# Routed experts of one fused transformer step: f32 products against three f16 products of two-part operands

## What is computed

```python
logits = xt @ gate_w.T
_, idx = jax.lax.top_k(logits + beta, K)                      # K = 2 of E = 8
probs = jax.nn.sigmoid(jnp.take_along_axis(logits, idx, axis=-1))
c = jnp.zeros((B, E), xt.dtype).at[jnp.arange(B)[:, None], idx].add(probs)
g = jnp.einsum('bh,ehm->bem', xt, gate_proj_w)
u = jnp.einsum('bh,ehm->bem', xt, up_proj_w)
h = jax.nn.silu(g) * u
eo = jnp.einsum('bem,emh->beh', h, down_proj_w)
combined = jnp.einsum('beh,be->bh', eo, c)                    # + the shared expert, every token
```

## Time and profile before

| | us |
|---|---|
| time before, median of 3 runs | 3458.92 (3457.98 to 3466.2) |
| span of the profiled execution | 3454.1 |
| PE busy in it | 3251.6 (94%) |
| DVE busy | 2715.8 (79%) |
| ACT busy | 2222.3 (64%) |
| POOL busy | 1600.3 (46%) |
| first stage, to its last product | 0 to 304 |
| second stage, from its first transpose to its last product | 312 to 756 |

### The profile page before, as it was taken

The page is one execution under the profiler, slowest core; times in us unless marked ns, Lnnn a source line. Parts: engine busy times, 40 slices in busy tenths (PEclk is TensorE's granted clock), DMA queues, the critical chain, the costliest instruction groups (busy, mean ns, idle before and its releaser), DMA issues. The chain is left out here.

```text
span 3454.1 us, 59006 instructions
## 1 busy us (share of the span) xinstructions
PE 3251.6 (94%) x19214; PEld 1316.3 (38%) x19215; DVE 2715.8 (79%) x4886; ACT 2222.3 (64%) x3468; POOL 1600.3 (46%) x2080
## 2 busy tenths in 40 slices
PE   8998999999999999999999999778999999999987
PEld 5655666652222222222222222252334334333333
DVE  5564222559999999999999999366989999898997
ACT  3331222127888888888878888757877777777763
POOL 2124000003444343344444443306888888887885
PEclk9999999999999999999999999988999999999998
DMA  4443111111121111111111110041222222222221
GB/s 156 133 163 114 47 45 44 42 42 30 35 60 41 39 38 33 31 32 31 34 36 35 35 36 23 30 141 59 71 74 69 82 73 69 74 83 69 76 77 50
DMA packets 160884, 211.56 MB, mean 61 GB/s; under 512 B 32324, under 2 KB 108364, under 8 KB 160604
## 3 DMA queue, kind: packets, MB, share of 16 engines
q1 hardware_dynamic: 141340, 172.51, 16.6%
q0 software_dynamic: 8512, 18.76, 1.7%
q10 hardware_dynamic: 10752, 16.78, 1.5%
HBM read 154.48 MB, written 52.69 MB: 60 GB/s over the span
## 5 line engine op out<-in xcount | busy, mean ns | idle before, releaser
L1289 ACT ACTIVATE prob<-psS 128x1024 f32<-128x1024 f32 (+3 forms) x1280 | 1104.1, 906 | 275.2 <-PE psS L1473 265.6
L1339 DVE TENSOR_REDUCE pmax<-psR 128x1 f32<-128x512 f32 x1674 | 1057.0, 684 | 76.9 <-PE psR L1415 46.6
L2115 POOL TENSOR_TENSOR hc<-h_d,crep 128x512 f32<-128x512 f32 x512 | 647.3, 1272 | 187.1 <-DVE h_d L2344 136.8
L1415 PE MATMUL psR<-kslab,qslab 48*128 48x512 bf16 (+3 forms) x2480 | 651.9, 351 | 22.2 <-DVE pmax L1339 13.8
L1488 PE MATMUL psVo<-prob,vaug 128*32 128x512 f32 (+3 forms) x5120 | 627.1, 543 | 1.7 <-ACT ov L1293 0.9
L1473 PE MATMUL psS<-qslab,kslab 51*128 51x512 bf16 (+3 forms) x2560 | 531.8, 352 | 39.5 <-ACT prob L1289 24.0
L2344 DVE TENSOR_TENSOR_SCAN h_d<-a,state,psU 128x512 f32<-128x512 f32 x384 | 489.4, 1275 | 0.0
L1204 POOL TENSOR_SCALAR_AFFINE_SELECT prob<-prob 128x256 f32<-128x256 f32 (+1 forms) x512 | 213.4, 420 | 529.0 <-ACT prob L1289 529.0
L1415 PEld LDWEIGHTS psR<-kslab,qslab 48*128 48x128 bf16 x2480 | 187.3, 94 | 627.9 <-DVE pmax L1339 468.7
L2334 DVE TENSOR_TENSOR psU<-dtx,psX 128x512 f32<-128x512 f32 x512 | 356.2, 696 | 88.9 <-PE psX L2494 38.5
L2247 ACT ACTIVATE a<-dt,a_neg 128x512 f32<-128x512 f32 x512 | 366.8, 724 | 53.8 <-DVE h_d L2344 53.0
(11 more groups left out here) (309 smaller groups left out, 4805.5 us busy)
## 6 DMA issues: line engine op xcount, KB each, us to landing
crep<-c_rows_d SPq DMA_DIRECT2D x256, 256.0 KB, 3.2
x_e<-rows_d SPq DMA_DIRECT2D x72, 128.0 KB, 2.0
y_d<-y SPq DMA_DIRECT2D x72, 128.0 KB, 1.7
q_d<-parts SPq DMA_DIRECT2D x48, 128.0 KB
k_d<-parts SPq DMA_DIRECT2D x48, 128.0 KB
qslab<-q_d SPq DMA_DIRECT2D x60, 96.0 KB
kslab<-k_d SPq DMA_DIRECT2D x60, 96.0 KB
x<-in_L_attn_x_dram SPq DMA_DIRECT2D x8, 512.0 KB, 6.3
```

The costliest lines, as they stand in the source:

```text
L1289: act.activation(prob[g % BUFS][:, :, off:BLK], psS[g % 2][:, :, off:BLK], ACT.Exp).then_inc(prob_ready, 1)
L1339: dve.tensor_reduce(into[:, lo:lo + (count - 1) * NEXT + 1:NEXT], psR[at % BANKS][:, 0:count * w].rearrange("p (n w) -> p n w", w=w), AX.X ...
L1415: ins = pe.matmul(dst[:, m * w:(m + 1) * w], qslab[u][rows, i * P:(i + 1) * P], kslab[u][rows, ch * BLK:ch * BLK + w], start=(m == 0), sto ...
L2115: pool.tensor_tensor(hc[:, g % CR], h[:, g % HR], crep[:, g // PAIR % SPR], ALU.mult).then_inc(hc_ready, 1)
```

## The change

Each f32 product of the routed experts becomes three f16 products: x and h are cut into a high and a low f16 part after their transpose, the weights in the first stage, and high*high + high*low + low*high is summed in PSUM. f16 needs a scale: each weight matrix is scaled by its own largest magnitude, x by 1024, and the factors are taken out again in SiLU's scale, in the product h and in the routing weights `c`.

In the first stage every block now handles one expert's weights. ACT loads them into one buffer `raw` (three DMAs, after `copy_values` of the block before, once POOL is through with the last ones). DVE takes their maxima (`weight_max`, ahead of `choose`), PE turns the maxima (`turn_max`, between the two first products), DVE builds a diagonal (`weight_row`), PE spreads it (`spread_max`, ahead of `product(u,0)`), DVE makes the scales (`weight_scale`). ACT writes the high parts and scales `raw` in place (six instructions of 128x1024 a block), and POOL subtracts to get the low parts (three of 128x1024 a block, `low_weights`, behind the scatters). `cut` has four instructions instead of five. x is loaded straight into `xn`. The zeros for the regions' tails are made by POOL after its last low part.

```diff
+            def low_weights(e):
+                for w, low in enumerate((keep["wgl"], keep["wul"], keep["wdl"])):
+                    high = (keep["wgh"], keep["wuh"], keep["wdh"])[w]
+                    pool.wait_ge(whigh_ready, 3 * e + w + 1 + CREDIT)
+                    pool.tensor_tensor(low[:, e].rearrange("p k m -> p (k m)"), raw[:, w],
+                                       high[:, e].rearrange("p k m -> p (k m)"), ALU.subtract).then_inc(wlow_ready, 1)
...
+                low_weights(n)
                 pool.wait_ge(scattered, 16 * 2 * TPB * (n + 1))
...
-                c.after(dve.tensor_tensor(rest[:], rest[:], parts[:, s, 1], ALU.subtract))
-                dve.tensor_copy(parts[:, s, 2], rest[:]).then_inc(parts_ready[s], 1)
+                dve.tensor_tensor(parts[:, s, 2], qf[:, s], parts[:, s, 1], ALU.subtract).then_inc(parts_ready[s], 1)
...
+            def weight_max(e):
+
+                dve.wait_ge(raw_in, 48 * e + 48 + CREDIT)
+                dve.tensor_reduce(wmax[:], raw[:], AX.X, ALU.max, apply_absolute_value=True).then_inc(wscale_step, 1)
...
             def load_expert(e):
+                act.wait_ge(wlow_ready, 3 * e + CREDIT)
...
+            def turn_max(e):
+                pe.wait_ge(wscale_step, 3 * e + 1 + CREDIT)
+                pe.wait_ge(y_ready, e + CREDIT)
+                pe.transpose(psWT, wmax[:], keep["ident"][:]).then_inc(wmax_moved, 1)
+
+            def spread_max(e):
+                pe.wait_ge(wscale_step, 3 * e + 2 + CREDIT)
+                pe.matmul(psWB, ones[0:3, :], diag_r[:], start=True, stop=True).then_inc(wmax_moved, 1)
...
             def step(i, s):
                 take_max(i, 0)
+                if known(i - 1, 0):
+                    dve.wait_ge(hTh_ready, i + CREDIT)
+                    dve.tensor_tensor(hTl[:, 1 - s], psH[:], hTh[:, 1 - s], ALU.subtract).then_inc(hTl_ready, 1)
+                if known(i + 1, 0):
+                    dve.wait_ge(xTh_ready, i + 2 + CREDIT)
+                    dve.scalar_tensor_tensor(out=xTl[:, 1 - s], in0=psX[:], scalar=X_TOP, in1=xTh[:, 1 - s],
+                                             op0=ALU.mult, op1=ALU.subtract).then_inc(xTl_ready, 1)
                 take_max(i, 1)
...
+            def split_products(dst, high, low, w_high, w_low, first, last):
+
+                pe.matmul(dst, high, w_high, start=first, stop=False)
+                pe.matmul(dst, high, w_low, start=False, stop=False)
+                return pe.matmul(dst, low, w_high, start=False, stop=last)
```

More of the change, by code:

```diff
@@ L423, in _ @@
             for n in range(NBLK):
+                weight_max(n)
                 choose(n)
                 cut(n, 0)
+                weight_row(n)
                 cut(n, 1)
@@ L560, in product @@
                     else:
[L561 removed]
+                        w = (wsg if kind == "g" else wsu)[:, k, x * P:(x + 1) * P]
                     ins = pe.matmul(psR[bank][:], w, xnT[n % 2][:, k], start=(k == 0), stop=(k == KD - 1))
@@ L594, in _ @@
                 product(n, "q", 0)
+                turn_max(n)
                 product(n, "q", 1)
                 product(n, "g", 0)
+                spread_max(n)
                 product(n, "u", 0)
@@ L665, in phase_experts @@
         psY = ps("psY", [P, D])
-        psM = ps("psM", [P, BLK])
+        MAX_BANKS = 3
+        psM = [ps(f"psM{s}", [P, BLK]) for s in range(MAX_BANKS)]
         qz = [sb(f"qz{a}", [P, T], BF16) for a in range(2)]
@@ L851, in step @@
                 take_max(i, 2)
-            steps(dve, step, -1, RT + 1)
-            lc = Chain(dve, lam_step)
+                if isinstance(i, int) and i == 2:
+                    scale_outputs()
+            steps(dve, step, -1, RT)
             dve.wait_ge(lam_load, 64 + CREDIT)
             lv = lam_in[:].rearrange("p (m w) d -> p m w d", w=2)
-            lc.after(dve.tensor_tensor(lam_w[:], lv[:, :, 0], lv[:, :, 1], ALU.mult))
-            lc.after(dve.tensor_reduce(lam_s[:], lam_w[:], AX.X, ALU.add))
+            fc.after(dve.tensor_tensor(lam_w[:], lv[:, :, 0], lv[:, :, 1], ALU.mult))
@@ L859, in _ @@
+            fc.after(dve.tensor_reduce(lam_s[:], lam_w[:], AX.X, ALU.add))
         @block.tensor
         def _(pe):
-            pe.wait_ge(keep["moe_w"], 16 * 3 * E)
             def max_product(i, slot):
@@ L913, in step @@
                     ins.then_inc(d_done, 1)
                 max_product(i, 2)
-                if known(i - 1, 0):
-                    pe.wait_ge(h_ready, i + CREDIT)
-                    if known(i - 1, 1):
-                        pe.wait_ge(hT_ready, i - 1 + CREDIT)
-                    for m in range(MT):
-                        ins = pe.transpose(psH[:, m], h[:, 1 - s, m * P:(m + 1) * P], keep["ident"][:])
-                    ins.then_inc(h_turned, 1)
-            steps(pe, step, -1, RT + 1)
+            steps(pe, step, -1, RT)
```

296 lines of the change are left out of this document (186 added, 110 removed).

## The result

The changed kernel takes **3516.0 us** (median of 4 runs, 3510.7 to 3522.3) against 3459.6 (4 runs, 3458.0 to 3466.2) for the kernel before, run beside it: ratio 1.0163, 95% interval 1.0145 to 1.0181. It is slower by 1.6%. Forecast were 3489 us, +0.9%, and a range that ended at 3512: the sign is right, the size is not.

What follows compares the result with a forecast made beforehand. PE was taken to set the pace in both edited stages. Profiled span 3454.1 + 64 + 2 + 43 - 79 = 3484 us; with the runs' median 4.8 above it, 3489 us (+0.9%), range 3434 to 3512.

Steps and rivals of the forecast that it cites:

- Second stage: Second stage's loop: f16 products shorten tiles to 4.6 us and steps with maxima to 5.6; -79 us in all.
- start and tail: Second stage's two ends: the start comes out even, the part after the last gate gains 3 us.
- The weights' load: First stage: PE waits 6.0 us a block for the weights' maximum, plus 3.2 for the spread; 9.2 x 7 = +64 us.
- the spread: First stage, PE's second wait, before spread_max: an extra 2.6 or 3.5 us a block, taken as 3.2.
- DVE's chain: First stage: choose, cut(0) and weight_row end 6.1 us after the maximum, against PE's two products of 3.5 us.
- the low clock: First stage, behind the wait for the maximum: PE's two products may not have the full clock; 3.5 us extra.
- The first block: First stage: the first block's load is issued at the start and competes with x's; +2 us.
- POOL beside DVE: First stage: POOL's low parts hold up DVE's cut(n,3) ahead of down; 5.4 x 8 = +43 us.
- the taking of turns: In cut(3), DVE and POOL instructions alternate: cast waits 1.1, subtraction 2.2, cast 2.2; 5.4 us a block.
- the hold-up: POOL's low parts delaying cut(3): full 38%; rivals none 27% (same sum without 43) and casts only 12% (23 us).

Runs made afterwards that it cites:

- e3: Changed kernel with both moves: next expert's load issued ahead of the copies, POOL's low parts behind hidden(n,3); 3430.8 us, ratio to the kernel before 0.9905.
- e11: e7 with the weights' maximum taken in two instructions, the first two thirds while the last third loads; 3389.2 us, ratio to the kernel before 0.9793.
- e1: Changed kernel with ACT issuing the load of expert n+1 before copy_shared(n) and copy_values(n), not behind them; 3466.1 us.
- e7: e6 with each load third issued after its own low part, turn_max behind the logits, weight_row ahead of choose, spread_max one product earlier; 3411.5 us.
- e4: Changed kernel with POOL waiting for each low part's own completion before it issues the next; 3513.6 us.
- e12: Changed kernel with the first cast of cut(n,3) made to wait for a tiny POOL memset right ahead of the low parts; 3524.1 us.
- e9: Changed kernel with six surplus products put into PE's wait before down, their output overwritten by down; 3497.0 us.
- e6: e3 with the tails' zeros in the free half of xn, not the weights' buffer, so tail stores don't wait for the last low parts; 3422.7 us.
- e8: Changed kernel with twelve surplus products put into PE's wait before down, their output overwritten by down; 3519.4 us.
- e2: Changed kernel with POOL's three low parts waiting until DVE has finished hidden(n,3); 3455.2 us.
- e5: Changed kernel with each of POOL's low parts written as two instructions of 512 columns, without a wait between them; 3525.8 us.
- e10: Changed kernel with the first cast of cut(n,3) written as eight casts of 64 columns; 3526.5 us.

## Why the prediction was right and where it failed

**Second stage, -79 forecast, -83.1 measured: right.** 4.69 us a tile against 4.6; 5.44 a step with maxima against 5.6; start and tail -7.0 against -3, since the last tiles run 4.2 us shorter, not 3, and the first three 2.8 shorter, not even.

**The weights' load, +64 forecast, 46.0 + 17.5 = 63.5 measured: right**, with the parts as worked out: the reduction took 3.35 us (3.5), all landed 6.6 us after the issue at 173.8 (5.5), PE waited 6.6 (6.0), the spread cost 2.5 (3.2). Of the two values that I gave for the spread, 2.6 for DVE's chain and 3.5 for the low clock, the first was the nearer: e3 shows 2.1 of the 2.5 with PE waiting at the full clock. The 3.5 was an estimate, that both products run at the low clock to their end, and no run shows it: behind the wait for `wmax` the granted clock is 0.50 for 2.8 to 6.0 us in the changed kernel (0.50 too in the kernel before from 310 to 318 us, between the two stretches of the earlier trace rows), and from the product on `wmax` to the one on `diag_r` are 5.75 to 6.61 us there and no more in any run, 2.1 to 3.0 above the 3.64 of e11. The first block lost 3.4, not 2. e1 shows that the 46.0 come from the place of the load. Most of the 17.5 doesn't: it came back there as the wait for `diag_r` (10.7 us), since `weight_row` stood behind `choose` and `cut(n,0)`, and went only with e7's order.

**POOL beside DVE, +43 forecast.** The idle time before `down` rose by 44.4 us, so the number held, but partly by accident: the taking of turns that I wrote ("cast waits 1.1, subtraction 2.2, cast 2.2") is what e4 shows, with gaps; in the changed kernel one instruction waits for all three, 6.4 us longer than alone, of which 5.5 reach PE. The low parts took 2.13 us each (2.2 assumed). The term was an estimate from the scatters' 1.21 us against 1.013, which are no arithmetic. The trace agrees with it in that one of the engines waits for whole instructions of the other, but not for one at a time: it shows 6.86 us for three in a row. The rows don't show that the order decides: in all eight blocks the held DVE instruction starts 0.04 to 0.28 us before POOL's first low part, and yet DVE is the one that waits. Starts on POOL are rough in a profile, so these distances say little by themselves, but in e12 the cast waits for a memset ahead of the low parts, starts 0.2 us behind the first of them, and is held as well (6.38 us).

One stage of the kernel before does have arithmetic on both engines, and I hadn't used it. In the last one 512 DVE products with one input in PSUM (`psU<-dtx,psX`, 128x512) run nearly all beside POOL's f32 products of 1.27 us, and none takes over 0.70 us. In e4's last block `hidden`, which also reads PSUM, takes its usual 0.69 beside a low part. What is held in these runs is casts and two-input instructions whose inputs all lie in SBUF.

**The step that failed is the missing term behind it.** For the wait for `wmax` I had asked what 6 us of idleness do to the granted clock, from the earlier trace rows, and priced the products behind it. For the wait before `down`, which my own sum made just as long (1.4 + 5.4 = 6.8 us), I asked nothing and took `down` at its 7.17 us. It took 10.05 in the block shown, 19.0 us more in all eight. e9 fills that wait and `down` loses 17.3 of the 19.0; that its median gains 19.1 is a coincidence, since only 14.3 of it arise before the second stage.

With 19.0 from there, 5.2 that I had entered at nothing (the sixteen small products, 3.8, and a remainder), 2.8 from the hold-up and the first block, and +11.7 in the later stages, against the second stage's 3.4 more of gain (-83.1 + 0.7 for its start, -79 forecast) and 0.5 on the load, the 3484 of the forecast span become the 3519 measured. By the medians the forecast was 27 us low, 4 us outside its range; the clock term alone would have brought it to 3508, inside it.

**The later stages, +11.7.** Their instructions are the same. 7.9 lie in the last stage, from its first product on `pick` to the end: 1104.9 us before, 1112.8 after. But this value follows no edit: it is 1104.8 to 1105.0 in the kernel before, e6, e8, e9 and e11, 1112.6 to 1113.1 in the changed kernel, e1, e2, e3, e5, e7 and e12, 1109.8 in e4 and 1111.3 in e10. It arises at three places of the stage, about 150, 287 and 693 us after its start, with 2 to 3.5 us each. At the first of them the same short waits of PE stand in both runs; then the clock is at 0.50 for some 3.4 us in one and for some 10 in the other (stretches of 2 us added up). Stretches of 20 us there, the same work in each (the number before the last two is the clock), kernel before and kernel after:

```profile
2489.20:2509.20 20.00, 17.33 (x80) 7.04 (x81) 18.61 (x21) 18.19 (x37) 14.93 (x13) 0.91 0.21 73
```
```profile
2546.20:2566.20 20.00, 17.86 (x67) 6.22 (x65) 17.42 (x20) 15.50 (x34) 14.32 (x12) 0.74 0.18 58
```

So about 8 us of any comparison of two profiled runs here can be this, and it is no cost of the change. It may be in the medians as well: the changed kernel's four times are 3510.7, 3511.4, 3520.7 and 3522.3, and the profiled one is the third; the others' stages weren't recorded. The other 3.9 lie between the first attention product and the last stage, 1588.7 us before and 1590.4 to 1593.6 in the changed kernel and every variant; I have not followed them.

**What decides the change.** The f16 products bring their 83 us; the way in which the weights were split gave back 135. With the split placed elsewhere (e11) it gives back about 9 (the second stage's first gate is at 322.8 against 313.7), and the same change is 2.1% faster.

## What to carry to other kernels

Price a wait of the engine that sets the pace twice: its length, and what the products behind it lose at the lower clock (0.50 here); 6.9 us of waiting cost 9.3 on average, 2.4 of them by the clock. Work put on an idle engine isn't free when it can hold up a neighbour on the critical chain (44.4 us of waiting before `down` here): place it where that neighbour idles, and look again at the last iteration, where something else may stand there. And before a transfer's wait is accepted, see whether its issue stands behind work that it doesn't depend on: moving it by two lines gave 50 us. Before an edit is credited with a gain, read the gain at the end of the stage that it touches: e6 gained 8 us and e9 some 5 in stages that they don't touch.

## What the runs showed of the hardware that I had not expected

- A DVE cast of 128x512 (0.42 us) beside POOL subtractions of SBUF tiles is held until a row of them without gaps is through: 6.86 us for three, a DVE subtraction 7.59 us for six half as long. With a semaphore wait between POOL's instructions DVE gets in after each (2.75, 2.49, 2.23 us). In `tables()` it got in without one; neither the length of the DVE instruction (64 columns: 6.98 us) nor the order of arrival (6.38 us) explains that.
- DVE instructions with one input in PSUM kept their 0.69 us beside POOL's arithmetic.
- Both sides wait: where DVE did get in, POOL's low part took 2.38 us instead of 2.12.
- After 6.9 us of idleness `down` took 8.8 to 10.2 us (granted clock 0.50 over the first 5 us of the 10.05). After 0.5 to 1.9 us it took 7.17 in all blocks of the kernel before, e2 and e9 but one (8.86). In e7 the products behind idle times of 1.4 to 2.0 us were slow in two cases of seven, so a short wait has no fixed price.
- One surplus f32 product of 128x512 costs 0.87 us at the full clock (1.00 in e8 and e9 while they ran), and 42.5 us of them brought the second stage 14.3 us forward.
